# A selective-scan kernel whose `w` products move to 64-row bands, two states per pass and interleaved by column

## The chip, the cores and the metric

The kernel runs as one program on one core of one Trainium2 chip. The metric is device time in microseconds (us), the median of several runs; less is better. TensorE, VectorE, ScalarE, GpSimd and the DMA engines work side by side and meet at semaphores.

## What is computed

A pre-norm block in two stages, all in fp32, on x of shape (2, 2048, 256): first a selective scan, then a routed mixture of eight experts.

```
x = x + scan_layer(layernorm(x))
x = x + experts(layernorm(x))          # argmax of 8 logits picks one expert per token

scan_layer: dt = softplus(...); A = -exp(log_A)              # D = 256 channels, N = 16 states
  h[t] = exp(dt*A) * h[t-1] + (exp(dt*A) - 1)/A * x[t] * B[t,n]
  y[t] = sum over n of h[t] * C[t,n]; return y + D_skip * x
```

The kernel rewrites the recurrence. With v[t] = x[t]·B[t,n] and w[t] = v[t] − v[t−1], it runs h' = (h' + w)·a, a = exp(dt·A), so that VectorE's scan instruction has two operands: `w`, and `a`. The `w` of a state n is a product on TensorE of x (tokens by channels) with a banded matrix that has B[t,n] on its diagonal and −B[t,n] one column to its right.

## The kernel before

**Chunks, items, pairs.** Tokens are worked in eight chunks q of 512 (TC), each in four blocks of 128 tokens (TI). Channels are two halves h of 128. An item is one state n of one half h, all 512 tokens: 32 items per chunk (ITEMS), 256 in all, numbered g. Before, item g of a chunk has n = g // 2 and h = g % 2, so a pair (`m`) is one state in both halves.

**The stations of an item.** GpSimd builds the band of a state (`make_band`, L555: 128 x 516, that is four blocks of 129 columns), which both halves share. TensorE makes `w` (`make_w`, L921): four products, one per block of tokens, each with a full 128-row weight load of x and 129 columns of band streamed past it, into one PSUM bank of 512 columns. The 129th column spills into the next block and accumulates there. Each fp32 product stands in the trace as two weight loads and two matmuls, so an item has eight. There are NW = 4 such banks, item g uses bank g % 4. ScalarE makes `a` (`exp_a`, L741). VectorE scans (`scan`, L1110). Then h is multiplied by C/A: for most items on GpSimd (`make_hc`, L574), for which the scan writes to SBUF and ScalarE has scaled a copy of C (`copy_C`, L730); for the items of the states in VECTOR_N on VectorE (L1130), for which the scan works in place in PSUM. TensorE turns the result and adds it into YY (`add_y`, L939), four transpositions per item.

**What sets the order.** Every engine has its own program, written out by hand. TensorE's `emit(q)` goes over n = 0..15. In step n it makes `w` of items 2m+4 and 2m+5 and adds y of items 2m−4 and 2m−3, where m = 16q + n. `w` of item g waits until item g−4 has left its bank: the scan of g−4 where GpSimd multiplies, VectorE's product where VectorE does. For n < 2 and for the states on VectorE the two `add_y` stand ahead of the two `make_w`, otherwise behind. One small job per step (`fill`, a "hop": the layer norms' transpositions, projections, skip terms, routing) stands between. The hop tables give the skip terms u01 and u23 to steps 13 and 14 (L874) and the route to step 11.

**What VectorE does between scans.** `between(j, gap)` places its other work behind scan j of a chunk: `finish_rows` of the chunk before (L1168, two instructions behind each of scans 4 and 5; it waits until all y of that chunk are added), `ln2_stats` (behind 6 and 7), `dt_add` (L1137, behind 20 and 27), and `u_times_x` (L1158, two instructions behind each of scans 28 and 30; they wait for hop u01 and hop u23). In the last chunk u01 and u23 are hops 3 and 4 and are read behind scans 9 and 11. Hop u01 itself waits for `dt_add` behind scan 27, whose bank it takes.

**The rest.** After the eight chunks the expert stage runs 39 tiles of 128 tokens (hidden layer L1008, output L1024); the change does not touch it. Before the first chunk TensorE runs 80 small bf16 products (L964) and 24 products of 64 rows and 129 columns, by turns in the upper and the lower half of the array and in two banks (L967).

## Time and profile before

| | us |
|---|---|
| median of 3 runs | 805.61 (805.4 to 806.9) |
| the profiled execution | 804.56, its span 802.8 |
| first chunk starts on ScalarE (L690) | 25.2 |
| hidden layer of the experts starts (L1008) | 479.2 |
| TensorE busy, VectorE busy, GpSimd busy, ScalarE busy | 749.1, 546.2, 533.0, 461.3 |

A row of a timeline gives start, duration, engine, source line, operation and the tiles written and read; rows in a run are merged with a count. TensorE has two lines: PE for the matmuls, PEld for the weight loads that run under them. A matmul's shown duration contains its way through the array, so that its rate is read from start to start. A window row gives the busy time of each engine in a stretch and the clock that TensorE was granted in it, 1.00 being 2.4 GHz and 0.50 being 1.2 GHz.

### The profile page before, as it was taken

How to read it: one execution, taken by the hardware profiler on the slowest of the kernel's cores; microseconds unless marked ns; L12 is line 12 of the kernel's file. 1: busy time of each engine (PE TensorE's matmuls, PEld its weight loads, DVE VectorE, ACT ScalarE, POOL GpSimd, SP SyncE). 2: the span in 40 equal slices, each digit the busy share in tenths (PEclk: the TensorE clock that was granted, in tenths of full speed). 3: DMA queues.
4: the chain of work that ended last, by engine and by line, in shares of the span. 5: the costliest groups of instructions: out<-in, count | busy, mean ns of one | idle time of the engine just before them, and what ended most of it. 6: DMA issues, size and time to landing. Idle time of an engine off the chain costs nothing. (4 is left out here: it accounts for less than half of the span.)

```text
span 802.8 us, 17303 instructions
## 1 busy us (share of the span) xinstructions
PE 749.1 (93%) x5642; PEld 695.0 (87%) x5643; DVE 546.2 (68%) x914; ACT 461.3 (57%) x941; POOL 533.0 (66%) x654
## 2 busy tenths in 40 slices
PE   7899999999999997998998975969999999999993
PEld 5799999999899897898897975959999999999992
DVE  6889998989989989989789963353333334333430
ACT  3777898887888876876866753422332233223330
POOL 2799999989989986999898863552333343334420
PEclk9799999999999999998999987989999999999997
DMA  8666643233323331642844448341111111111000
GB/s 290 198 220 233 259 135 105 94 132 106 124 76 106 134 106 54 122 112 60 124 90 54 165 137 283 34 54 40 50 46 53 39 44 49 43 55 53 23 9 0
DMA packets 44375, 82.49 MB, mean 103 GB/s; under 512 B 6280, under 2 KB 14733, under 8 KB 44304
## 3 DMA queue, kind: packets, MB, share of 16 engines
q1 hardware_dynamic: 38288, 68.98, 29.2%
q0 software_dynamic: 6016, 12.61, 6.4%
q8 instruction: 38, 0.62, 0.3%
q14 instruction: 33, 0.27, 0.1%
HBM read 70.41 MB, written 13.91 MB: 105 GB/s over the span
## 5 line engine op out<-in xcount | busy, mean ns | idle before, releaser
L574 POOL TENSOR_TENSOR w_sb<-w_sb,Csb 128x512 f32<-128x512 f32 x182 | 231.7, 1275 | 41.2 <-DVE w_sb L1110 28.5
L921 PE MATMUL WW<-b_sb,xin 128*128 128x129 f32 (+1 forms) x1536 | 206.3, 284 | 8.3 <-DVE w_sb L1130 5.8
L921 PEld LDWEIGHTS WW<-b_sb,xin 128*128 128x128 f32 x1536 | 190.2, 197 | 24.0 <-issue 13.8
L812 ACT ACTIVATE dt<-WW,b1c 128x128 f32<-128x128 f32 x312 | 89.1, 369 | 191.8 <-PE WW L1008 191.8
L1110 DVE TENSOR_TENSOR_SCAN w_sb<-WW,hlast,w_sb 128x512 f32<-128x512 f32 x138 | 173.3, 1271 | 17.6 <-PE WW L921 17.2
L741 ACT ACTIVATE w_sb<-dt,negA 128x512 f32<-128x512 f32 x256 | 170.9, 710 | 18.7 <-DVE w_sb L1110 15.0
L1024 PE MATMUL misc<-w_sb,dt 128*128 x624 | 146.8, 390 | 9.1 <-issue 9.1
L634 POOL DMA_INDIRECT y_out<-CbX,ocol x39 | 46.8, 1201 | 150.5 <-DVE CbX L1418 149.9
L1024 PEld LDWEIGHTS misc<-w_sb,dt 128*128 128x128 f32 x624 | 119.5, 197 | 25.9 <-issue 10.1
L939 PE MATMUL YY<-sm,w_sb 128*128 128x128 f32 x1024 | 129.3, 276 | 0.1
L1008 PE MATMUL WW<-z,xin 128*128 128x128 f32 x624 | 120.7, 275 | 0.0
L939 PEld LDWEIGHTS YY<-sm,w_sb 128*128 128x128 f32 x1024 | 117.3, 144 | 0.3 <-POOL w_sb L574 0.3
L555 POOL TENSOR_TENSOR b_sb<-sm,brow 128x516 f32<-128x516 f32 x96 | 101.1, 1054 | 0.3
L730 ACT ACTIVATE Csb<-w_sb,invA 128x512 f32<-128x512 f32 x126 | 85.9, 713 | 26.4 <-POOL w_sb L574 26.2
L1415 DVE TENSOR_TENSOR CbX<-misc,b_sb 128x256 f32<-128x256 f32 x39 | 16.6, 425 | 118.0 <-PE misc L1024 118.0
L1008 PEld LDWEIGHTS WW<-z,xin 128*128 128x128 f32 x624 | 96.1, 192 | 0.9
L921 PEld LDWEIGHTS WW<-band,xin 128*128 128x128 f32 x512 | 63.2, 195 | 19.4 <-issue 10.8
L921 PE MATMUL WW<-band,xin 128*128 128x129 f32 (+1 forms) x512 | 68.7, 282 | 11.5 <-DVE w_sb L1130 11.5
L1110 DVE TENSOR_TENSOR_SCAN WW<-WW,hlast,w_sb 128x512 f32<-128x512 f32 x54 | 66.3, 1269 | 4.4 <-ACT w_sb L741 3.4
L1008 PE MATMUL WW<-z,xnT 128*128 128x128 f32 x320 | 62.0, 276 | 0.0
L1008 PE MATMUL WW<-z,Csb 128*128 128x128 f32 x304 | 58.8, 275 | 0.0
L1110 DVE TENSOR_TENSOR_SCAN w_sb<-WW,w_sb 128x512 f32<-128x512 f32 x44 | 52.9, 1212 | 5.6 <-PE WW L921 5.5
(214 smaller groups left out, 880.0 us busy)
## 6 DMA issues: line engine op xcount, KB each, us to landing
w_sb<-c_rows SPq DMA_DIRECT2D x86, 256.0 KB, 3.7
CbX<-c_rows SPq DMA_DIRECT2D x42, 256.0 KB, 3.5
w_sb<-w_in SPq DMA_DIRECT2D x20, 512.0 KB, 5.7
token_rows<-row SPq DMA_DIRECT2D x8, 1024.0 KB, 5.0
w_sb<-w_in SPq DMA_DIRECT2D x24, 256.0 KB, 6.6
xin<-x_in SPq DMA_DIRECT2D x8, 512.0 KB, 4.1
...
```

The lines of the kernel that those rows point to most:

```text
L555: eng.tensor_tensor(bands[m % NR], col("band").unsqueeze(1).to_broadcast([P, TI, BAND]), brow[q % B][:, :, N + n:N + n + 1].to_broadcast([ ...
L574: eng.tensor_tensor(hc[g % NHC], hb_of(g), Csb[i % NCS][:, :], ALU.mult).then_inc(s_hcp, 1)
L634: eng.indirect_dma_start(out=outrows, out_offset=bass.IndirectOffsetOnAxis(ap=ocol[u][:, :], axis=0), in_=yo[u], in_offset=None, bounds_ch ...
L730: eng.activation(Csb[i % NCS][:, :], Cb[m % NB], ACT.Copy, scale=invA[:, h * N + n:h * N + n + 1])\
L741: eng.activation(A[g % NA], dts[q % B][:, h * TC:(h + 1) * TC], ACT.Exp, scale=negA[:, h * N + n:h * N + n + 1]).then_inc(s_a, 1)
L812: g = eng.activation(hT[u % 2][:, j * P:(j + 1) * P], hps[u % 2][:, j * P:(j + 1) * P], ACT.Gelu, bias=b1c[u][:, j:j + 1])
L921: mm = eng.matmul(bank_of_w[:, i * P:i * P + width], x_rows[:, i, h * P:(h + 1) * P], bands[m % NR][:, i, 0:width], start=(i == 0), stop=( ...
L939: mm = eng.matmul(YY[:, at:at + P], hc[g % NHC][:, i * P:(i + 1) * P], ident, is_transpose=True, start=(j == 0 and i % 2 == 0), stop=(j == ...
L1008: mm = eng.matmul(hps[u % 2][:, j * P:(j + 1) * P], w1c[u % 2][h][:, j * P:(j + 1) * P], xT[u % 2][:, h * P:(h + 1) * P], start=(h == 0), ...
L1024: mm = eng.matmul(yps[u % 2][:, 0:D], hT[u % 2][:, j * P:(j + 1) * P], w2_sb[:, bass.ds(e * KH * D + j * D, D)], start=(j == 0), stop=(j = ...
L1110: eng.tensor_tensor_scan(hb_of(g) if pooled(g) else bank[g % NW], bank[g % NW], A[g % NA], hlast[(q - 1) % 2][:, h * N + n:h * N + n + 1] ...
L1415: eng.tensor_tensor(yo[u], yps[u % 2][:, 0:D], b2_sb[:, bass.ds(e * D, D)], ALU.add)\
```

## The change

Items are renumbered (`place`): a unit is now two neighbouring states n, n+1 of one half h, four items being (n, h0), (n+1, h0), (n, h1), (n+1, h1). A band is cut into blocks of 64 tokens and holds both states column by column: per 128 tokens 65 x 2 = 130 columns, so that one band of 128 x 520 serves four items. `w` of a unit lies interleaved in two PSUM banks (two units at a time, 1024 columns each), and the scan and VectorE's product read and write it at every second column. `make_w(m, part)` makes a unit in two parts. Part 0 has products of rows 0 to 63 into the first bank and of rows 64 to 127 into the second, by turns, and at its end one product of 2 columns for the spill across the bank's edge; part 1 has the halves the other way round, behind a wait for part 0. One `add_y` stands between the parts and one behind, the hop comes last, and all steps have this one order. On VectorE both products of a unit stand behind its second scan. VectorE's share goes from 37 pairs to 27 units; GpSimd's rises from 182 to 202 items.

```
-VECTOR_N = [(1, 3, 5, 8, 11, 13)] + [(1, 5, 8, 11)] * 4 + [(1, 3, 5, 8, 11)] * 2 + [(1, 4, 7, 10, 13)]
+VECTOR_UNITS = [(1, 6, 9, 12)] + [(1, 6, 11)] * 6 + [(1, 4, 7, 10, 13)]
-BAND = P + 1
-NR, NA, NH, NHC, NCS, NW, NB = 4, 4, 8, 8, 3, 4, 6
+HALF = P // 2
+BAND = 2 * (HALF + 1)
+NR, NA, NH, NHC, NCS, NW, NB = 3, 4, 8, 8, 3, 4, 6
...
+def place(g):
+    q, j = divmod(g, ITEMS)
+    return q, j // 4 * 2 + j % 2, j // 2 % 2
...
+        def unit(m):
+            return WW[:, m % 2 * 1024:(m % 2 + 1) * 1024]
+
+        def w_of(g):
+            return unit(g // 2).rearrange("p (t s) -> p s t", s=2)[:, g % 2, :]
...
-                eng.tensor_tensor(bands[m % NR], col("band").unsqueeze(1).to_broadcast([P, TI, BAND]),
-                                  brow[q % B][:, :, N + n:N + n + 1].to_broadcast([P, TI, BAND]), ALU.mult)\
-                   .then_inc(s_R, 1)
+                eng.tensor_tensor(bands[pair % NR].rearrange("p i (t s) -> p i t s", s=2),
+                                  col("band").unsqueeze(1).unsqueeze(3).to_broadcast([P, TI, HALF + 1, 2]),
+                                  brow[q % B][:, :, N + 2 * p:N + 2 * p + 2].unsqueeze(2)
+                                  .to_broadcast([P, TI, HALF + 1, 2]), ALU.mult).then_inc(s_R, 1)
...
+            def make_w(m, part):
...
+                pair, h = divmod(m, 2)
+                x_rows, band, to = xin[m // N % B], bands[pair % NR], unit(m)
+
+                def product(r, k, at=0, width=BAND, start=False):
+                    rows = slice(HALF * r, HALF * r + HALF)
+                    a = 2 * (P * k + HALF * r) + at
+                    return eng.matmul(to[:, a:a + width], x_rows[rows, k, h * P:(h + 1) * P],
+                                      band[rows, k, at:at + width], start=start, stop=not start, skip_group_check=True)
+
+                if part == 0:
+                    if h == 0:
+                        eng.wait_ge(s_R, pair + 1)
+                    if m >= 2:
+                        if pooled(2 * m - 4):
+                            eng.wait_ge(s_h, 2 * m - 2)
+                        else:
+                            eng.wait_ge(s_hc, vector_before(2 * m - 2))
+                    product(0, 0, start=True)
+                    product(1, 2, start=True)
+                    product(0, 1)
+                    product(1, 3, width=2 * HALF)
+                    product(1, 1, at=2 * HALF, width=2).then_inc(s_wf, 1)
+                else:
+                    eng.wait_ge(s_wf, m + 1)
+                    product(0, 2)
+                    product(1, 0)
+                    product(0, 3)
+                    product(1, 1, width=2 * HALF).then_inc(s_wv, 2)
...
-                    if n < 2 or n in VECTOR_N[q]:
...
+                    make_w(m + 2, 0)
+                    add_y(KD * m - 4)
+                    make_w(m + 2, 1)
+                    add_y(KD * m - 3)
+                    if n in at:
+                        fill(*at[n])
...
-                    if g % KD and not pooled(g) and KEPT[g // KD]:
-                        keep_h(g)
-                    if g and not pooled(g - 1):
+                    if g % KD and not pooled(g):
                         make_hc(g - 1)
+                        if KEPT[g // KD]:
+                            keep_h(g)
+                        make_hc(g)
```

How instructions stand on the engines, at three places. First TensorE in chunk 3, step 13, where hop u01 (two products of 17 rows, `misc<-sm,z`) stands; `h_ready` counts scans, `hC_ready` VectorE's products, `hC_ready_gpsimd` GpSimd's. Before:

```order
L921 MATMUL WW<-band,xin 128x129 [waits h_ready,band_ready]
L921 MATMUL WW<-band,xin 128x129 x2
L921 MATMUL WW<-band,xin 128x128
L874 MATMUL misc<-sm,z 128x256 [waits shared_bank_read_by_scalar,dt_ready]
L874 MATMUL misc<-sm,z 128x256
L921 MATMUL WW<-band,xin 128x129 [waits h_ready]
L921 MATMUL WW<-band,xin 128x129 x2
L921 MATMUL WW<-band,xin 128x128
```

and the same step after the change:

```order
L936 MATMUL WW<-b_sb,xin 128x130 [waits h_ready]
L936 MATMUL WW<-b_sb,xin 128x130 x2
L936 MATMUL WW<-b_sb,xin 128x128
L936 MATMUL WW<-b_sb,xin 128x2
L972 MATMUL YY<-sm,w_sb 128x128 [waits hC_ready]
L972 MATMUL YY<-sm,w_sb 128x128 x3
L936 MATMUL WW<-b_sb,xin 128x130 [waits w_of_first_halves]
L936 MATMUL WW<-b_sb,xin 128x130 x2
L936 MATMUL WW<-b_sb,xin 128x128
L972 MATMUL YY<-sm,w_sb 128x128 [waits hC_ready]
L972 MATMUL YY<-sm,w_sb 128x128 x3
L892 MATMUL misc<-sm,z 128x256 [waits shared_bank_read_by_scalar,dt_ready]
```

The hop stood behind one item's four products, which wait for scan 26; it now stands behind a whole unit and two `add_y`, and the first of these products waits for scan 27. On VectorE the reader of the hop (`tail<-misc`) stands where it stood, one scan behind `dt_add`; the rows of the changed kernel in chunk 1, where L1135 is the scan:

```order
L1135 SCALAR_TENSOR_TENSOR w_sb<-WW,hlast,w_sb 128x512 [waits hC_ready_gpsimd,a_ready,w_ready]
L1161 SCALAR_TENSOR_TENSOR dt<-misc,mag 128x512 [waits softplus_log]
L1135 SCALAR_TENSOR_TENSOR w_sb<-WW,hlast,w_sb 128x512 [waits h_last_kept,hC_ready_gpsimd,a_ready,w_ready]
L1182 SCALAR_TENSOR_TENSOR tail<-misc,vns,xin 128x256 [waits rstd_ahead,z_ready,shared_bank_filled]
L1182 SCALAR_TENSOR_TENSOR tail<-misc,vns,xin 128x256
L1135 SCALAR_TENSOR_TENSOR w_sb<-WW,hlast,w_sb 128x512 [waits hC_ready_gpsimd,a_ready,w_ready]
```

Here nothing moved. Last, TensorE in step 1 of chunk 4, where the last two y of chunk 3 are added. Before, the two `add_y` stand ahead, then a small hop, then `w`:

```order
L939 MATMUL YY<-sm,w_sb 128x128 [waits hC_ready_gpsimd]
L939 MATMUL YY<-sm,w_sb 128x128 x3
L869 MATMUL misc<-sm,cbrow 17x128 [waits cb_rows_ready,shared_bank_read_by_scalar]
L869 MATMUL misc<-sm,cbrow 17x128 x3
L921 MATMUL WW<-band,xin 128x129 [waits hC_ready,band_ready]
```

and after:

```order
L936 MATMUL WW<-b_sb,xin 128x130 [waits hC_ready]
L936 MATMUL WW<-b_sb,xin 128x130 x2
L936 MATMUL WW<-b_sb,xin 128x128
L936 MATMUL WW<-b_sb,xin 128x2
L972 MATMUL YY<-sm,w_sb 128x128 [waits hC_ready_gpsimd]
L972 MATMUL YY<-sm,w_sb 128x128 x3
L936 MATMUL WW<-b_sb,xin 128x130 [waits w_of_first_halves]
L936 MATMUL WW<-b_sb,xin 128x130 x2
L936 MATMUL WW<-b_sb,xin 128x128
L972 MATMUL YY<-sm,w_sb 128x128 [waits hC_ready_gpsimd]
L972 MATMUL YY<-sm,w_sb 128x128 x3
```

The last y of a chunk, for which `finish_rows` waits, now stands behind both parts of a `w` that itself waits for VectorE's products of unit 1.

## Rows read from the trace of the kernel before

**Rows 1.** The page's first part: busy us, share of the span, instructions.
```profile
PE 749.1 (93%) x5642; PEld 695.0 (87%) x5643; DVE 546.2 (68%) x914; ACT 461.3 (57%) x941; POOL 533.0 (66%) x654
```
**Rows 2.** Windows, one per chunk: us, busy us per engine (instructions), PE clock, DMA.
```profile
25.20:80.50 55.30, 51.38 (x390) 47.40 (x391) 49.38 (x58) 43.03 (x73) 51.51 (x68) 0.94 0.66 222
80.50:134.90 54.40, 54.22 (x446) 50.43 (x446) 50.54 (x66) 46.19 (x80) 50.17 (x59) 1.00 0.47 167
...
243.50:297.30 53.80, 53.75 (x445) 50.21 (x444) 49.34 (x71) 46.06 (x79) 48.69 (x58) 1.00 0.33 106
297.30:359.70 62.40, 58.17 (x463) 54.12 (x464) 57.06 (x80) 45.87 (x79) 52.70 (x61) 0.97 0.45 105
359.70:419.00 59.30, 55.66 (x429) 51.63 (x427) 51.97 (x77) 45.12 (x78) 55.48 (x64) 0.94 0.52 92
419.00:479.00 60.00, 52.49 (x412) 49.09 (x413) 53.59 (x78) 38.57 (x62) 49.02 (x52) 0.95 0.43 110
```
**Rows 3.** Groups by line of the whole span: count, busy us, mean ns, idle before.
```profile
L574 POOL TENSOR_TENSOR w_sb<-w_sb,Csb 128x512 f32<-128x512 f32 x182 | 231.7, 1275 | 41.2 <-DVE w_sb L1110 28.5 <-ACT Csb L730 11.7 <-PE misc L874 0.7
L1110 DVE TENSOR_TENSOR_SCAN w_sb<-WW,hlast,w_sb 128x512 f32<-128x512 f32 x138 | 173.3, 1271 | 17.6 <-PE WW L921 17.2
...
L555 POOL TENSOR_TENSOR b_sb<-sm,brow 128x516 f32<-128x516 f32 x96 | 101.1, 1054 | 0.3
```
**Rows 4.** Timeline of weight loads in chunk 3, 225 to 243 us: start, us, operation.
```profile
229.65 3.65 PEld L921 LDWEIGHTS WW<-b_sb,xin 128*128 128x128 f32 x32
233.23 0.91 PEld L939 LDWEIGHTS YY<-sm,w_sb 128*128 128x128 f32 x8
234.10 0.97 PEld L921 LDWEIGHTS WW<-band,xin 128*128 128x128 f32 x8
```
**Rows 5.** Timelines at the 64-row warm-up products, 7 to 10.5 us, and behind them.
```profile
7.62 2.95 PE L967 MATMUL WW<-tail 64*128 64x129 f32 x48
...
10.18 0.39 PE L967 MATMUL WW<-tail 64*128 64x129 f32 x4
...
10.50 0.14 PEld L845 LDWEIGHTS misc<-sm,xin 128*128 128x128 f32 x1
```
**Rows 6.** Timelines into and out of one skip-term hop, 184.7 to 186 us.
```profile
184.72 0.27 PE L921 MATMUL WW<-b_sb,xin 128*128 128x128 f32 x1
184.92 0.18 PEld L874 LDWEIGHTS misc<-sm,z 17*128 17x128 f32 x1
...
185.67 0.37 PE L874 MATMUL misc<-sm,z 17*128 17x256 f32 x1
185.98 0.19 PEld L921 LDWEIGHTS WW<-b_sb,xin 128*128 128x128 f32 x1 [0.33 <-issue]
```
**Rows 7.** Timeline of VectorE, 176 to 200 us: start, us, operation, count [idle before].
```profile
179.61 0.67 DVE L1137 SCALAR_TENSOR_TENSOR dt<-misc,mag 128x512 f32<-128x512 f32 x1
...
182.18 0.88 DVE L1158 SCALAR_TENSOR_TENSOR tail<-misc,vns,xin 128x256 f32<-128x256 f32 x2 [0.71 <-PE misc L874]
182.97 2.45 DVE L1110 TENSOR_TENSOR_SCAN w_sb<-WW,hlast,w_sb 128x512 f32<-128x512 f32 x2
...
192.77 0.72 DVE L1130 SCALAR_TENSOR_TENSOR w_sb<-WW,invA,w_sb 128x512 f32<-128x512 f32 x1
...
195.25 0.86 DVE L1168 SCALAR_TENSOR_TENSOR row<-YY,mvx,tail 128x256 f32<-128x256 f32 x2
...
199.18 0.72 DVE L1064 BATCH_NORM_STATS2 st<-row 128x6 f32<-128x256 f32 x2
```
**Rows 8.** Windows of 4 us in chunk 0: us, busy us per engine, PE clock, DMA.
```profile
28.00:32.00 4.00, 1.67 (x16) 1.38 (x15) 3.96 (x5) 1.76 (x4) 3.92 (x8) 1.00 0.62 197
32.00:36.00 4.00, 3.49 (x19) 3.26 (x18) 3.12 (x4) 4.00 (x8) 3.06 (x3) 0.54 0.37 88
```
**Rows 9.** Timeline at 477 us: two bf16 products of 96 columns, the second written strided.
```profile
477.23 0.29 PE L893 MATMUL misc<-onehot,tri_bf 128*128 128x96 bf16 x1
...
477.32 0.36 PE L894 MATMUL misc<-onehot,ones_bf 128*128 128x96 bf16 x1
```

130 lines of the change are left out of this document (51 added, 79 removed).

## The prediction

> **What bounds the kernel now.** First the page's busy line [rows 1]: TensorE is busy 93% of the span, VectorE 68%, but that is a mean over two stages. The change lies in the scan stage, 25 to 479 us, so I read the windows by chunk [rows 2]. In chunks 1 to 4 TensorE is busy all but 0.2 us of 54.4 us or less and VectorE 49 to 51: there TensorE is the bound. In chunks 5, 6 and 7 all of TensorE, VectorE and GpSimd are at 80 to 94% of their 59 to 62 us and wait for each other, and the clock is granted at 0.94 to 0.97. Then the pace of TensorE: an instruction of `w` comes every 3.58/32 = 0.112 us, one of y every 0.87/8 = 0.109 us [rows 4]. A unit of two items is 16 of the one and 8 of the other: 1.79 + 0.87 = 2.66 us, 42.6 us per chunk; the other 11.8 us of 54.4 are hops.
>
> **The concurrency is real.** The 24 warm-up products of 64 rows, by turns in the two halves and two banks, are the new `w` in small. Their 48 instructions take 2.88 us to the next kind's first load [rows 5]; without the way in and out (below) that is 0.055 us each, half of 0.112. So a part of four products costs 8 x 0.055 + 0.06 for the last to end = 0.50 us, two parts 1.00 instead of 1.79.
>
> **What the parts pay for it.** Each part is entered from and left to full-height work. The trace shows such borders. Into a hop of 17 rows: the last full matmul starts at 184.72, ends its columns 0.11 later (the step of [rows 4]), the next load starts only at 184.92 instead of under it, and takes another 0.11 until columns flow at 185.03: 0.20 lost. Out of it: 256 columns, twice as many, end at 185.67 + 0.21, load at 185.98, columns at 186.09: 0.20 [rows 6]. Out of the 64-row products into transpositions: the last matmul starts at 10.18 + 0.39 − 0.27 = 10.30, its columns end 0.11 later, the load comes at 10.50 and is 0.05 shorter: 0.15 [rows 5]. Every unit has four such borders: 2 x 0.20 + 2 x 0.15 = 0.70 us. The Trainium skill has this as a rule ("TensorEngine Tiling (Array Packing)", Key Properties: changing the tiling mode drains TensorE) without a price; the same page promises up to twice the speed for 64 rows, and by that alone a unit would lose 0.8 us.
>
> The product of 2 columns: its two instructions lie between 0.02 us (nothing but columns) and 0.22 us (two ordinary ones, 0.112 each). Its first load runs under the matmul ahead and its second doesn't, so I take 0.13.
>
> Sum for a unit on TensorE: 1.00 + 0.70 + 0.13 + 0.87 = 2.70 us against 2.66. The halving is eaten by the borders. Three hops per chunk are short-row work that now begins or ends at a 64-row part and saves a border each, 0.5 us. TensorE per chunk: 16 x 2.70 + 11.8 − 0.5 = 54.5 us, as before.
>
> **GpSimd.** 64 bands fewer at 1.054 = −67.5 us, 20 multiplications more at 1.275 = +25.5 us [rows 3]: 42 us less in the stage. The new band has 4 elements more but runs of two; no row shows that form. Between 1.05 us and the 1.28 us of a product with two full operands [rows 3]; I take 1.06. In either case GpSimd isn't the bound in chunks 1 to 4, and the gain counts in 5 to 7 only. ScalarE gets 20 copies of 0.71, 1.8 us per chunk, on 46 of 54 [rows 2]: hidden.
>
> **VectorE.** 20 products less; a scan steps on by 1.22 us, a product by 0.65, a skip-term pair takes 0.79, a `finish_rows` pair 0.78, statistics 0.65, `dt_add` 0.58 [rows 7] (shown times less the 0.07 to 0.09 by which neighbours overlap). About 1.3 us per chunk less. Scans and products now read every second column of PSUM. No row shows VectorE doing so. A scan takes 1.27 us for 512 columns, where the product, which reads the same bank, takes 0.72 [rows 3, 7]; a scan doesn't read PSUM as fast as it can be read, so I take no change; the bound on the other side is under the rivals.
>
> **The looser grip.** Before, `w` of an item waits for the item four back; from `w` ready to the next use of its bank TensorE has three items' work, about 5 us, and VectorE needs 1.2 of it. Now a unit waits for the unit two back, both scans done. From TensorE's start of a unit to `w` ready is about 2.3 us (part 0 0.6, border and y 0.6, border and part 1 0.7, the array 0.2, semaphores and first load 0.2), then VectorE takes 2.4; the bank is wanted again after 2 x 2.70 plus hops. That leaves 0.7 us where no hop stands. Any VectorE work above it stops TensorE. Three places per chunk do:
>
> 1. Start of a chunk. Unit 1 is VectorE's own and takes 2.4 + 1.3 + 0.1: 0.3 us of stop. Then the last y of the chunk before comes 2.9 us after unit 1 is done (all of step 1); VectorE has done scan 4 after 1.2 and waits 1.7 for it in `finish_rows`. Unit 2 is thus done at 2.9 + 0.8 + 1.2 = 4.9 us; TensorE was free at 2.7 + 0.4 for its hop: 1.8 idle. Unit 3 takes 0.8 + 1.2 + 0.65 + 1.2 = 3.85 against TensorE's 2.70: 1.15 idle; unit 4 another 0.2. Together 3.5 us.
> 2. Hop u01. It comes 2.7 + 1.05 + 0.15 = 3.9 us after scan 27. VectorE is there after `dt_add` and scan 28, 1.8 us, and waits 2.1 or more (0.71 before [rows 7]). TensorE has nothing else to do until scan 29: 0.8 + 1.2 + 0.05 = 2.05 idle.
> 3. Hop u23 and scan 31, the same: 2.05.
>
> That is 7.6 us per ordinary chunk, less the 0.2 that TensorE idles now. What hides none of it: after each of these points TensorE's next instruction in order is the `w` that waits.
>
> **Sum**, against the profiled execution's 804.6 us. Chunks 1 to 4: 4 x (7.4 + 0.1) = +30. Chunk 5: 54.5 + 7.5, and 2.2 more because token placing falls on unit 1, gives 64.2 against 62.4: +1.8. Chunk 6: 62 against 59.3: +2.6. Chunk 0 has no `finish_rows` and no route, but u01 and u23 (+4.1), less about 1.6 of waits for VectorE's own products, which are two states fewer: +2.5. Chunk 7 has its skip terms early, where no stop follows, pays the start (3.5) and gains from a lighter GpSimd: −1. The expert stage is unchanged. 804.6 + 36 = 840.5; the median stood 1 us above the profiled execution, so 840 to 841. **Forecast 840 us, slower by 4%.**
>
> **Rivals.**
> (a) Borders cost nothing here, because neighbouring loads slip under. A unit is 2.0 us, TensorE 43 us per chunk, and VectorE bounds: its 48 busy, 1.3 + 2.0 us of waits for the hops, 1 for `finish_rows`, some 2.5 behind long hops, 55 us. Chunks 1 to 4 stay within +1, chunks 5, 6 and 7 fall to about 58, 56 and 55, chunk 0 by 2: 805.6 − 10 = 796. Against it: two kinds of border in the rows show 0.15 to 0.20. This is the case on the faster side; it decides from a border below about 0.08 us. Chance 0.20.
> (b) Borders of half that: 2.35 per unit, chunks near 57 to 58: 805 to 822. 0.12, nearly all of it slower.
> (c) The forecast, 822 to 850: 0.48.
> (d) The new idle stretches let the clock fall. In chunk 0 TensorE was busy 1.67 of 4 us and the next 4 us ran at 0.54 of full speed, near 1.2 GHz [rows 8]. The stops at u01 and u23 leave it busy some 60% over 8 us, which is better than that. If it falls once in each chunk, 2 to 3 us each: 860. 0.12.
> (e) Strided PSUM reads slow the scan. The nearest row is TensorE's second bf16 product, 0.36 us for 96 columns written at a stride against 0.29 [rows 9], 0.7 ns per column. On 512 columns 0.37 us per scan, 12 us of VectorE per chunk, half of it beside TensorE: 885. The Trainium skill ("Advanced Engine Details and Errata", PSUM Cachelines) says that access to PSUM that isn't contiguous slows matmuls down much; of VectorE it says nothing. 0.06.
> (f) The halves don't overlap in the real `w` (same operands, real data): 16 x 0.112 + 0.70 + 0.13 + 0.87 = 3.5 us per unit, 13 us more per chunk than in (c): 940. 0.02.
>
> Faster by over 0.2%: (a) and a little of (b), 0.22; within 0.2%, about what a measurement can tell from no change, 0.04; slower 0.74. The range from 796 to 862 takes in (a) to (d) but for their ends.
>
> **What the changed profile would show.** Loads of the 64-row parts 0.055 apart, and a gap of 0.2 us at each change to and from y; if there is none, (a). A unit's 2.7 us from start to start in the middle of a chunk. VectorE waiting for TensorE 2 to 3 us ahead of each skip-term pair and 1.7 us ahead of `finish_rows` (by L1182 and L1192); if these are under 1 us, points 1 to 3 are wrong. Scans still 1.27 us, bands near 1.06. TensorE's clock at 1.00 in the middle of chunks. The stage's end near 515 us instead of 479, and the expert stage as long as before. The forecast is wrong above all if TensorE runs ahead at these places in a way that I missed, or if the two-column product costs more.

## The result: 13% slower, three times the loss that was forecast

The changed kernel takes 916.91 us (median of four runs, 904.6 to 925.7) against 805.51 for the kernel before. The times of the runs below are medians too, while the ratios leave out the slower executions of a kernel as a rule: the ratio here is 1.1285 (95% interval 1.1182 to 1.1387), by medians it is 1.138. The forecast was 840 with a range up to 862, so the sign was right and the size was not. The profiled execution is the fastest of the four, 904.62 us. In the four the time rises as the mean granted clock falls (0.877, 0.863, 0.856, 0.850), the first hint that the clock has a share in the loss.

The page's first part, to be read beside [rows 1]:

```profile
PE 791.9 (88%) x5898; PEld 667.1 (74%) x5899; DVE 535.2 (59%) x885; ACT 471.5 (52%) x961; POOL 495.2 (55%) x619
```

The windows, one per chunk and one for the expert stage, as in [rows 2] (us; busy us and instructions of TensorE, its loads, VectorE, ScalarE, GpSimd; clock; DMA):

```profile
25.70:94.80 69.10, 59.50 (x438) 46.31 (x438) 48.10 (x53) 45.81 (x77) 51.86 (x69) 0.75 0.60 201
94.80:162.20 67.40, 57.83 (x478) 45.37 (x478) 49.17 (x62) 47.15 (x81) 44.54 (x53) 0.89 0.35 119
162.20:230.70 68.50, 59.16 (x478) 46.57 (x478) 50.02 (x63) 47.17 (x81) 45.57 (x54) 0.87 0.26 86
230.70:301.30 70.60, 61.26 (x478) 48.31 (x478) 49.16 (x59) 47.19 (x82) 41.62 (x39) 0.84 0.25 83
301.30:373.00 71.70, 63.21 (x478) 49.76 (x478) 49.90 (x70) 47.05 (x81) 44.59 (x53) 0.81 0.26 82
373.00:446.00 73.00, 61.20 (x480) 48.11 (x480) 51.64 (x70) 47.28 (x81) 51.00 (x59) 0.83 0.31 81
446.00:514.40 68.40, 58.76 (x478) 46.38 (x478) 52.58 (x78) 47.45 (x82) 53.28 (x62) 0.87 0.35 79
514.40:578.00 63.60, 55.68 (x424) 45.43 (x424) 48.48 (x67) 37.13 (x61) 35.27 (x38) 0.80 0.36 111
578.00:902.80 324.80, 294.17 (x1990) 274.37 (x1990) 118.69 (x291) 96.16 (x322) 120.82 (x169) 0.96 0.21 55
```

The expert stage is as long as before (324.8 against 802.8 − 479.2 = 323.6). Nearly all of the loss lies in the chunks: 67 to 72 us in chunks 1 to 4 where before they took 54, and the clock is granted at 0.81 to 0.89 where it was 1.00 [rows 2]. No other engine is the bound: none is busy for more than 53.3 us of any chunk.

The groups that answer to [rows 3]. GpSimd's product and VectorE's scan are what they were, the new band takes 1.065 us against 1.054:

```profile
L593 POOL TENSOR_TENSOR w_sb<-w_sb,Csb 128x512 f32<-128x512 f32 x202 | 255.4, 1272 | 169.0 <-DVE w_sb L1135 111.6 <-ACT Csb L749 24.9 <-PE YY L972 13.3
L1135 DVE TENSOR_TENSOR_SCAN w_sb<-WW,hlast,w_sb 128x512 f32<-128x512 f32 x152 | 188.9, 1269 | 29.8 <-issue 28.6 <-PE WW L936 0.5
L574 POOL TENSOR_TENSOR b_sb<-sm,brow 128x520 f32<-128x520 f32 x64 | 68.1, 1065 | 0.4
```

The weight loads of one unit at 2.4 GHz, chunk 2 (start, us): part 0, y, part 1, y, and the next hop, to be read beside [rows 4]:

```profile
203.28 0.75 PEld L936 LDWEIGHTS WW<-b_sb,xin 64*128 64x128 f32 x10 [1.06 <-DVE w_sb L1154]
204.04 0.42 PEld L972 LDWEIGHTS YY<-sm,w_sb 128*128 128x128 f32 x4
204.63 0.53 PEld L936 LDWEIGHTS WW<-b_sb,xin 64*128 64x128 f32 x8 [0.17 <-issue]
205.27 0.42 PEld L972 LDWEIGHTS YY<-sm,w_sb 128*128 128x128 f32 x4
205.66 1.87 PEld L903 LDWEIGHTS misc<-sm,xnrT 128*128 128x128 f32 x16
```

2.38 us from the first load to the hop, and 0.17 to 0.2 more where a half follows instead: 2.6 us, where 2.70 was forecast. The halves do run side by side.

The waits of VectorE in the scan stage, 26 to 578 us (total, times, longest), by the line that waited:

```profile
DVE tail L1182 <- PE misc L892: 53.3, 15, 5.8
...
DVE row L1192 <- PE YY L972: 18.7, 7, 4.4
```

And the end of chunk 2, TensorE and VectorE; then the clock in windows of 4 us over the same stretch:

```profile
214.27 1.13 PE L892 MATMUL misc<-sm,z 17*128 17x256 f32 x4
215.43 0.88 DVE L1182 SCALAR_TENSOR_TENSOR tail<-misc,vns,xin 128x256 f32<-128x256 f32 x2 [3.96 <-PE misc L892]
...
217.64 0.83 PE L936 MATMUL WW<-b_sb,xin 64*128 64x130 f32 x10 [2.25 <-DVE w_sb L1135]
...
223.19 0.88 DVE L1182 SCALAR_TENSOR_TENSOR tail<-misc,vns,xin 128x256 f32<-128x256 f32 x2 [4.51 <-PE misc L892]
...
225.31 1.45 PE L936 MATMUL WW<-b_sb,xin 64*128 64x130 f32 x10 [2.16 <-DVE w_sb L1135]
```

```profile
214.00:218.00 4.00, 1.75 (x14) 1.15 (x13) 2.57 (x4) 0.86 (x2) 0.42 (x1) 1.00 0.20 64
218.00:222.00 4.00, 4.00 (x27) 3.17 (x25) 0.67 (x1) 2.31 (x4) 3.24 (x4) 0.65 0.00 0
222.00:226.00 4.00, 1.84 (x9) 1.03 (x9) 2.81 (x4) 0.00 (x0) 0.67 (x1) 0.50 0.10 26
226.00:230.00 4.00, 4.00 (x26) 3.43 (x24) 2.58 (x3) 0.00 (x0) 4.00 (x5) 0.50 0.48 175
230.00:234.00 4.00, 4.00 (x27) 3.58 (x25) 2.69 (x4) 3.29 (x7) 0.21 (x1) 0.50 0.00 0
```

The stops stand where the prediction put them: VectorE waits for u01, then TensorE stands 2.25 us; the same at u23. But behind the first one the clock goes to 1.2 GHz, and it stays there for 16 us. At that clock a unit takes 4.6 us (255.03 to 259.67 in the trace of e3, below), and VectorE waits longer for the next hop: in chunks 0 to 5 it waits 3.9 to 5.8 us for u23. For u01, ahead of the fall, it waits 2.5 to 2.7 us, as forecast; only in chunk 2, the one shown, is it 3.96, and there a first short stretch at 1.2 GHz (208 to 212 us) lies ahead of it, right behind the route hop (205.8 to 207.5).

To compare kernels I counted the windows of 2 us with a clock under 0.75 in the scan stage: how many stretches of them, how long together, and the longest. The kernel before has 4 stretches, 26 us in all, the longest 8. The changed kernel has 16, 186 us in all, the longest 26.

### The profile page after: what moved, and what is told of

It is laid out like the page before. It is cut to its first block and busy times, and to the rows that moved or that the text cites. A ratio compares the mean times of both kernels' runs of the same rounds, so it can differ in the third digit from the quotient of the medians.

```text
span 902.8 us, 17676 instructions
## 1 busy us (share of the span) xinstructions
PE 791.9 (88%) x5898; PEld 667.1 (74%) x5899; DVE 535.2 (59%) x885; ACT 471.5 (52%) x961; POOL 495.2 (55%) x619
## 5 line engine op out<-in xcount | busy, mean ns | idle before, releaser
L593 POOL TENSOR_TENSOR w_sb<-w_sb,Csb 128x512 f32<-128x512 f32 x202 | 255.4, 1272 | 169.0 <-DVE w_sb L1135 111.6
L936 PEld LDWEIGHTS WW<-b_sb,xin 64*128 64x128 f32 x2304 | 196.6, 221 | 143.8 <-issue 91.4
L936 PE MATMUL WW<-b_sb,xin 64*128 64x130 f32 (+2 forms) x2304 | 234.6, 326 | 74.3 <-DVE w_sb L1135 63.6
L1135 DVE TENSOR_TENSOR_SCAN w_sb<-WW,hlast,w_sb 128x512 f32<-128x512 f32 x152 | 188.9, 1269 | 29.8 <-issue 28.6
L972 PE MATMUL YY<-sm,w_sb 128*128 128x128 f32 x1024 | 193.6, 320 | 0.0
L972 PEld LDWEIGHTS YY<-sm,w_sb 128*128 128x128 f32 x1024 | 124.6, 157 | 20.4 <-issue 6.5
L1050 PEld LDWEIGHTS misc<-w_sb,dt 128*128 128x128 f32 x624 | 119.3, 196 | 26.1 <-issue 10.5
L574 POOL TENSOR_TENSOR b_sb<-sm,brow 128x520 f32<-128x520 f32 x64 | 68.1, 1065 | 0.4
L1135 DVE TENSOR_TENSOR_SCAN w_sb<-WW,w_sb 128x512 f32<-128x512 f32 x50 | 59.0, 1208 | 12.1 <-issue 7.5
L1135 DVE TENSOR_TENSOR_SCAN WW<-WW,hlast,w_sb 128x512 f32<-128x512 f32 x40 | 50.1, 1281 | 17.8 <-ACT w_sb L759 9.1
L749 ACT ACTIVATE Csb<-CbX,invA 128x512 f32<-128x512 f32 x66 | 44.9, 711 | 15.3 <-POOL w_sb L593 15.1
L1034 PEld LDWEIGHTS WW<-z,xnT 128*128 128x128 f32 x320 | 49.8, 192 | 1.6 <-issue 0.8
```

The costliest lines, as they stand in the source:

```text
L574: eng.tensor_tensor(bands[pair % NR].rearrange("p i (t s) -> p i t s", s=2), col("band").unsqueeze(1).unsqueeze(3).to_broadcast([P, TI, HA ...
L593: eng.tensor_tensor(hc[g % NHC], hb_of(g), Csb[i % NCS][:, :], ALU.mult).then_inc(s_hcp, 1)
L749: eng.activation(Csb[i % NCS][:, :], Cb[m % NB], ACT.Copy, scale=invA[:, h * N + n:h * N + n + 1])\
L936: return eng.matmul(to[:, a:a + width], x_rows[rows, k, h * P:(h + 1) * P], band[rows, k, at:at + width], start=start, stop=not start, ski ...
L972: mm = eng.matmul(YY[:, at:at + P], hc[g % NHC][:, i * P:(i + 1) * P], ident, is_transpose=True, start=(j == 0 and i % 2 == 0), stop=(j == ...
L1034: mm = eng.matmul(hps[u % 2][:, j * P:(j + 1) * P], w1c[u % 2][h][:, j * P:(j + 1) * P], xT[u % 2][:, h * P:(h + 1) * P], start=(h == 0), ...
```

## The experiments

**Theory at the start:** the stops named in the prediction, made dearer by the clock that falls behind them. **Rivals:** the borders of the half-array work or the two-column product cost more than taken; VectorE's waits hide something that is late anyway. Ratios are to the kernel before on the same chip, since its own time there was between 804 and 814 us. The last three columns are of the one execution that was traced.

| kernel | ratio (95%) | by medians | traced, us | shortest of chunks 1 to 4, its clock | at 1.2 GHz: stretches, us, longest |
|---|---|---|---|---|---|
| before | 1 | 1 | 804.6 | 53.8, 1.00 | 4, 26, 8 |
| changed | 1.128 (1.118 to 1.139) | 1.138 | 904.6 | 67.4, 0.89 | 16, 186, 26 |
| e1 hops first | 1.080 (1.069 to 1.090) | 1.078 | 864.0 | 58.3, 0.97 | 13, 152, 44 |
| e2 y first | 1.093 (1.083 to 1.103) | 1.103 | 912.4 | 67.2, 0.86 | 13, 222, 30 |
| e3 both | 1.018 (1.012 to 1.024) | 1.027 | 845.6 | 58.3, 0.94 | 9, 116, 42 |
| e4 filler | 1.117 (1.109 to 1.124) | 1.111 | 888.8 | 62.8, 1.00 | 10, 118, 26 |
| e5 full height | 1.118 (1.114 to 1.122) | 1.119 | 903.4 | 65.8, 1.00 | 16, 66, 8 |
| e7 before, new order | 1.058 (1.054 to 1.062) | 1.060 | 854.9 | 61.5, 1.00 | 2, 16, 8 |
| e8 parts together | 1.030 (1.026 to 1.033) | 1.031 | 833.0 | 56.3, 1.00 | 8, 78, 18 |
| e10 lighter VectorE | 1.032 (1.024 to 1.040) | 1.031 | 826.8 | 55.6, 1.00 | 7, 86, 22 |
| e11 full height, both | 1.033 (1.028 to 1.038) | 1.032 | 831.7 | 58.9, 1.00 | 2, 8, 6 |
| e12 route later | 1.052 (1.048 to 1.057) | 1.053 | 853.4 | 61.2, 0.94 | 11, 110, 16 |

### e1 to e3: take the stops away

e1 puts hops u01 and u23 ahead of the step's first part:

```
+                    first = q + 1 < NQ and n in (13, 14)
+                    if first:
+                        fill(*at[n])
                     make_w(m + 2, 0)
...
-                    if n in at:
+                    if n in at and not first:
                         fill(*at[n])
```

> The changed kernel, but hops u01 and u23 stand ahead of the first part of w in steps 13 and 14 instead of behind the whole step; nothing else. Changed kernel: 917 us (905 to 926 in its runs). Theory T (stops of TensorE, with the clock falling to 1.2 GHz behind them): the waits of VectorE ahead of the skip terms (L1182, 53 us in all) fall under 15 us, the half-clock stretch at the end of each chunk shrinks, and the time falls by more than the 2 x 2.05 x 7 = 29 us of the stops themselves: to 850 to 880. Rival 1 (the borders of the array mode or the two-column product cost the excess, not the stops): 885 to 890 at best, since only the stops go. Rival 2 (VectorE's waits there are filled by work that is late anyway): no change, above 905.

Measured: 877.3 us (864.0 to 885.6), inside theory T's 850 to 880. VectorE's wait ahead of the skip terms falls from 53.3 to 10.9 us, and the shortest chunk takes 58.3 us with the clock at 0.97. Time at 1.2 GHz falls less, from 186 to 152 us, so these two stops aren't all that brings the clock down.

e2 puts both `add_y` ahead in steps 0 and 1:

```
+                    if n < 2:
+                        add_y(KD * m - 4)
+                        add_y(KD * m - 3)
                     make_w(m + 2, 0)
-                    add_y(KD * m - 4)
+                    if n >= 2:
+                        add_y(KD * m - 4)
```

> The changed kernel, but in steps 0 and 1 of a chunk both add_y stand ahead of the two parts of w; nothing else. Theory T: the wait ahead of finish_rows (18.7 us in all) falls under 5 us, TensorE's stops at units 2 to 4 shrink from 3.5 to about 1.5 us per chunk, and the time falls by 7 x 2 to 7 x 5 us, to 880 to 900, the more since the clock comes back earlier. Rival 1 (border costs): 903 or more. Rival 2: y ahead now holds w back (it waits for GpSimd's products) and the stop only moves: 910 to 925.

Measured: 897.5 us (882.7 to 912.4), inside theory T's 880 to 900 by its median. The wait ahead of `finish_rows` falls from 18.7 to 2.2 us; that ahead of the skip terms rises to 66.4.

e3 is both.

> Both of the two edits above. Theory T: the three stops of a chunk that the prediction named are gone or small, the clock stays near 2.4 GHz through chunks 1 to 4, chunks fall from 67 to 73 us to about 56 to 58: 805 to 835 in all. Rival 1 (the excess lies in the borders and in w itself): chunks stay above 62 us, 870 or more. The edits together should give more than the sum of the two alone if the clock needs both stops gone.

Measured: 836.1 us (825.7 to 845.6), VectorE's wait ahead of the skip terms down from 53.3 to 10.7 us and ahead of `finish_rows` from 18.7 to 1.3. Theory T had 805 to 835, rival 1 870 or more. Against the changed kernel e1 takes 0.049 off the ratio, e2 0.036, together 0.085; both edits in one kernel take 0.111 (by medians 0.060, 0.036 and 0.111). So each of the two orders holds part of the loss; that they make each other dearer is likely by the ratios and not clear by the medians. The rival by which the excess lies in borders and in `w` itself falls: e3 has all of these, and of the loss of 12.8% there are 1.8% left (2.7% by medians, of 13.8%). Two windows of e3's traced execution, 845.6 us and so above its median, show what is left. Chunk 2 takes 58.25 us at a clock of 0.94, chunk 3 takes 71.5; this is chunk 3 cut in two:

```profile
206.80:243.00 36.20, 31.78 (x300) 24.90 (x299) 30.49 (x38) 31.67 (x56) 26.55 (x26) 1.00 0.33 104
243.00:278.30 35.30, 35.30 (x181) 27.88 (x180) 19.28 (x23) 15.63 (x26) 16.69 (x16) 0.52 0.19 60
```

300 instructions of TensorE in the first 36 us, 181 in the next 35. In the second piece TensorE is busy without a gap, and the clock stays at 1.2 GHz from 244 us to the chunk's end.

### e4: keep the order, hold the clock up

Small bf16 products into a free bank, where TensorE stands still, in chunks 0 to 4. No other instruction's wait changes; those of steps 14 and 15 wait themselves until VectorE has read the bank.

```
+            def busy(b, q, n):
...
+                for i in range(24 if n > 3 else 16):
+                    eng.matmul(misc[b][:, 0:P], ones_bf[:, :], ones_bf[:, :], start=True, stop=True)
...
+                    if q < 4 and n in (14, 15):
+                        busy(0 if n == 14 else 1, q, n)
+                    if 0 < q < 5 and n in (2, 3):
+                        busy(1, q, n)
```

> The changed kernel in its own order, with small bf16 products (24 or 16 of 128 columns, into a free bank) put where TensorE stands still: ahead of steps 14 and 15 in chunks 0 to 3 and of steps 2 and 3 in chunks 1 to 4. They change no wait and no result. 24 of them take 1.3 us at 2.4 GHz and 2.6 at 1.2. If the clock is the missing term (T): it stays higher in chunks 1 to 4, and these fall from 67 to 73 us towards 62 to 64: 885 to 900 in all. If the clock is no cause, or idle time of 2 us doesn't lower it: the same or up to 10 us slower than the changed kernel, 915 to 930.

Measured: 904.6 us (888.8 to 912.9), between the two expectations, 885 to 900 and 915 to 930; the ratio is 1.117 against 1.128, by medians 1.111 against 1.138, and the traced execution takes 888.8 us where that of the changed kernel took 904.6. In all that is little, since chunk 4 has few fillers, chunks 5 to 7 none and the expert stage none, but the chunks with them separate the two parts of the loss. Chunks 1 to 3, then chunk 5, which has none:

```profile
90.35:155.37 65.02, 59.84 (x558) 47.64 (x559) 49.34 (x63) 47.26 (x82) 44.51 (x54) 0.95 0.43 138
155.37:218.15 62.78, 56.79 (x558) 45.69 (x559) 49.44 (x63) 47.28 (x82) 44.52 (x54) 1.00 0.30 94
218.15:282.13 63.98, 58.29 (x558) 46.66 (x558) 49.13 (x60) 47.23 (x81) 42.80 (x41) 0.97 0.26 92
...
349.73:423.87 74.14, 63.24 (x480) 49.94 (x480) 51.66 (x70) 47.36 (x82) 51.11 (x59) 0.80 0.30 79
```

With the clock at 1.00 the changed kernel's chunk takes 62.8 us. The prediction's sum for it was 61.9 (54.4 + 7.4 + 0.1). VectorE's waits with the clock held are those of the prediction too: 2.60 and 2.72 us ahead of that chunk's skip terms, 1.56 ahead of its `finish_rows`, which stands in the next chunk:

```profile
207.02 0.88 DVE L1194 SCALAR_TENSOR_TENSOR tail<-misc,vns,xin 128x256 f32<-128x256 f32 x2 [2.60 <-PE misc L892]
212.98 0.88 DVE L1194 SCALAR_TENSOR_TENSOR tail<-misc,vns,xin 128x256 f32<-128x256 f32 x2 [2.72 <-PE misc L892]
...
224.39 0.88 DVE L1204 SCALAR_TENSOR_TENSOR row<-YY,mvx,tail 128x256 f32<-128x256 f32 x2 [1.56 <-PE YY L972]
```

So of the changed kernel's 67.4, 68.5 and 70.6 us in chunks 1 to 3, some 62.8 is structure (order, units and borders at full clock) and 4.6 to 7.8 is the clock.

### e5: the same stops, full height

```
-                    rows = slice(HALF * r, HALF * r + HALF)
+                    rows = slice(0, P)
```

> The changed kernel, but every product of w takes all 128 rows instead of 64: the same number of products, columns, parts and waits, no change of the array's mode at the parts' edges, and no work side by side. The output is wrong (a block of w gets the sum over 128 tokens, not 64); only the time counts. By the rows of before a unit is 16 x 0.112 + 0.13 + 0.87 = 2.79 us on TensorE against 2.60 in the changed kernel's trace. In the runs so far the stretches at 1.2 GHz were 12 to 42 us long with the halves, though TensorE was busy in all of them, and 4 to 8 us in the kernel before. Theory C (work in halves, or its borders, keeps the clock down once it is down): the stops at the hops and at the chunk's start stay, but the clock returns within 4 to 8 us behind each, and the time is 860 to 890, below the changed kernel's 917 in spite of more work per unit. Theory S (the stops alone keep it down, whatever the work): the clock is as low as in the changed kernel, and 0.2 us more per unit give 930 to 950.

Measured: 902.6 us (899.4 to 903.9), neither theory's number. On the clock it sides with theory C: the stops are all there (1.81, 2.25 and 2.16 us in each of chunks 1 and 2), 16 times the clock falls, but no stretch is longer than 8 us and the clock is 0.93 to 1.00 in chunks 1 to 4. The same stops don't always bring it down: the chunk at 1.00 has all three. On the time theory C was 13 to 43 us too low; it had not counted that with the clock back the stops still cost what they cost. At the full clock the two can be compared: 65.8 us for a chunk here, 62.8 in e4. Halving is worth 3.0 us per chunk, 0.19 per unit, as long as the clock stays. The total says what it is worth with the clock: 1.118 at full height, 1.128 in halves, with intervals that overlap (by medians 1.119 and 1.138). It gives nothing, and costs 1 to 2% if the middles are right.

### e7: the old `w`, the new order

The kernel before, with `w`, y, `w`, y, hop in every step:

```
+                    make_w(KD * m + 4)
+                    add_y(KD * m - 4)
+                    make_w(KD * m + 5)
+                    add_y(KD * m - 3)
+                    if n in at:
+                        fill(*at[n])
```

> The kernel before with the step order of the changed one: w, y, w, y, hop, in every step. No halves, items and grip as before. Theory: w of an item waits there for one scan and not for two, with four items of reach, so the late hops and the late last y cost less: 1 to 3 us per chunk, 815 to 835 us with before at 806 to 814, and the clock comes back within 8 us of each stop. Rival: the order alone makes the change's loss: 870 or more. Second rival: no loss at all, then the stops need the unit of two states.

Measured: 854.4 us (851.7 to 854.9), more than the theory's 815 to 835 and less than the first rival's 870. Two of its chunks:

```profile
86.77:149.28 62.51, 56.23 (x445) 50.25 (x445) 51.12 (x66) 46.31 (x79) 49.93 (x59) 1.00 0.43 146
149.28:211.79 62.51, 56.23 (x445) 50.24 (x445) 51.12 (x66) 46.32 (x79) 49.97 (x59) 1.00 0.30 94
```

62.5 us at 1.00, where the kernel before takes 54.4 [rows 2] and the changed one with its clock held 62.8. The order by itself, without units, halves or the grip of two units, costs 8.1 us in chunks 1 and 2 and 7.3 and 7.7 in chunks 3 and 4. That is about as much as the changed kernel loses by structure, 8.4. And the clock stays at 1.00 in chunks 1 to 6, although TensorE is idle for 5.4 to 10.3 us of each. These aren't the stops of the changed kernel: behind u01 and u23 TensorE stands 0.63 us here, where it stood 2.25 and 2.16, and the longest stop of an ordinary chunk is 1.69. But chunk 5 has stops of 2.37, 1.46, 1.69 and 1.96 us within 14 us (they end at 340.0, 343.0, 347.6 and 351.6), and the clock holds there as well. So a stop of this length doesn't bring the clock down by itself.

### e8, e10, e12: can the halves be made to pay?

e8 is e3 with the two parts back to back and both `add_y` behind, so two borders per unit instead of four.

```
                     make_w(m + 2, 0)
-                    if n >= 2:
-                        add_y(KD * m - 4)
                     make_w(m + 2, 1)
                     if n >= 2:
+                        add_y(KD * m - 4)
                         add_y(KD * m - 3)
```

> The kernel with both edits (hops u01 and u23 first, y first in steps 0 and 1; 836 us), and in all steps the two parts of w back to back, then both add_y. Two borders per unit instead of four, 0.35 us less per unit by the prediction, but the wait for part 0 is then open: its last product's way through the array, about 0.2 us. If borders cost what the prediction took and hold the clock down: 815 to 832. If the wait costs as much as the borders: 832 to 842, no change. If y so late starves GpSimd's buffers: slower.

Measured: 831.4 us (828.7 to 833.0). That is where the two expectations meet (815 to 832, and 832 to 842 for no change). Against e3 it is no gain: 1.030 and 1.018 by the ratio, 1.031 and 1.027 by medians. The undisturbed chunks are shorter, 56.3 us at 1.00, and three of the eight at 64 us lose it again.

e10 gives unit 1 to GpSimd in chunks 1 to 6:

```
-VECTOR_UNITS = [(1, 6, 9, 12)] + [(1, 6, 11)] * 6 + [(1, 4, 7, 10, 13)]
+VECTOR_UNITS = [(1, 6, 9, 12)] + [(6, 11)] * 6 + [(1, 4, 7, 10, 13)]
```

> The kernel with parts together and both edits (831 us), and in chunks 1 to 6 only units 6 and 11 on VectorE, unit 1 on GpSimd too. VectorE's start of a chunk is 1.3 us shorter and TensorE's first unit waits for scans alone; GpSimd gets 2.55 us more on 45 of 56. If the grip of VectorE on TensorE at the chunk's start is what is left: 1 to 2 us per chunk and a better clock, 815 to 826. If GpSimd's buffers now hold VectorE back there: 831 or slower.

Measured: 829.0 us (823.2 to 834.2), above the 815 to 826 expected and by the ratio no better than e8. Chunks at full clock take 55.6 to 56.1 us, 0.7 less than in e8, and chunks 2, 5 and 6 fall to the low clock. Chunks 2 and 3:

```profile
137.32:200.56 63.24, 58.21 (x478) 47.12 (x477) 48.51 (x60) 48.07 (x83) 47.58 (x57) 0.87 0.30 93
200.56:256.17 55.61, 50.65 (x478) 41.23 (x477) 47.74 (x57) 47.82 (x83) 44.56 (x42) 1.00 0.31 105
```

The same work, 7.6 us apart by the clock. All three falls came within 4 us of the start of the route hop, whose sixteen instructions stream 8 columns each and which stands 6 us behind a stop of 1.6 us; in chunks 1, 3 and 4 the same stop and the same hop bring no fall. The first fall of e3 (128 us, its hop at 124.8) and three of e8 (the first at 184.9, its hop at 181.9) stand there too, while the kernel before runs this hop in chunks 1 to 4 without a fall. e12 moves it a step on:

```
-            at |= {8: ("xnr0", q - 1), 9: ("xnr1", q - 1), 11: ("route", q - 1)}
+            at |= {8: ("xnr0", q - 1), 9: ("xnr1", q - 1), 12: ("route", q - 1)}
```

> The kernel of e10 (parts together, both edits, lighter VectorE; 829 us), with the route hop (16 products of 8 columns, 1.85 us) in step 12 instead of step 11. In e10's trace the clock fell in chunks 2, 5 and 6 right behind this hop, which came 6 us after a stop of 1.6 us at dt_add; the chunks in which it didn't fall take 55.6 us, the others 63 to 67. If the stop and the short products together make it fall: it falls in fewer chunks, 805 to 822. If only the stop or only the hop does: no change, 825 to 835. Even at 2.4 GHz throughout it would not be under the kernel before, since 55.6 us is above its 54.4.

Measured: 853.2 us (850.4 to 864.7), slower than e10 and outside both expectations. VectorE reads the route behind scan 26 and now waits 2.67 us for it; hop u01, which waits for VectorE's `dt_add`, holds TensorE 2.5 us more; the clock falls in each of chunks 1 to 6, within 1 us of this new stop's end. The stop of 1.6 us is still there too, so this run doesn't tell what made the clock fall in e10. And even e10's best chunk, 55.6 us, is above the 54.4 of before: with these two-unit banks TensorE and VectorE, 50.7 and 47.7 us busy, still wait for each other. No version with halves beat the kernel before.

### e11: both edits, full height

> The kernel with both edits (hops first, y first; 836 us), but every product of w at full height, as in e5 (a wrong sum in w, the same counts and waits). A unit costs 0.2 us more at 2.4 GHz. Theory C (halves with their borders don't bring the clock back): the clock is 0.96 or more in chunks 1 to 4 and no stretch at 1.2 GHz is longer than 8 us; chunks 57 to 59 us, 825 to 840 in all, no slower than the halves in spite of more work. If halves cost no clock once the stops are gone: 6 x 16 x 0.2 = 20 us or more slower than e3, 855.

Measured: 830.4 us (829.9 to 831.7), as theory C expected. The edit is that of e5 on e3. Chunks 1 to 4 take 58.9 to 59.5 us, all at 1.00, and there are two low stretches of 8 us together in the whole stage, against 116 in the trace of e3. But the two kernels don't have the same stops: with its dearer units e11 has none above 0.68 us in chunks 1 to 4, while e3 still has stops of 1.04 to 1.64 us there, and in chunk 3 the clock falls behind the one of 1.57. So this pair doesn't tell whether the halves or the stops that they leave take the clock; only e5 against the changed kernel, with equal stops, speaks for the halves. By medians the halves (836.1 with before at 813.9, 1.027) and full height (830.4 with before at 804.3, 1.033) are about 0.5% apart, and by the ratios of the table 1.5%, at most 12 us; at a clock that held, 3.0 us per chunk would give 24. So half or more of what halving earns is lost again even with both orders mended.

### e6, e9, e13: the clock and the borders by themselves

Four, five and five tests on TensorE alone, each behind a stop. Their program is a list of calls; the halves and the full-height parts are those of the kernel:

```
+            stop(1)
+            for i in range(40):
+                halves_part(0)
+            stop(2)
+            for i in range(24):
+                halves_part(0)
+                turns()
...
```

> The changed kernel with four tests on TensorE put before the first chunk, each behind a stop of about 5 to 10 us: 40 parts in halves without anything between; 24 times a part in halves and four transpositions; 24 parts at full height, and right behind them, at whatever clock they leave, 24 times the mix of halves and transpositions; 20 times a part at full height and four transpositions. Theory C1 (halves alone keep the clock down): the first test stays at 1.2 GHz for over 10 us. Theory C2 (the borders do): the first test gets to 2.4 GHz as fast as the full-height one, the mix doesn't. Theory S: all four get to 2.4 GHz after the same few us. If a mix entered at 2.4 GHz stays there for 30 us, halves don't lower the clock, they only fail to bring it back. At 2.4 GHz the mix gives the price of a border: a part and four transpositions of 0.50 + 0.44 us without borders, 1.29 with the predicted 0.35. The time is not compared.

Measured: all four tests were back at 2.4 GHz 4.5 to 6.1 us after TensorE went to work again, and the mix that was entered at 2.4 GHz stayed there for its 30 us. In this run halves neither lower the clock nor keep it down, as theory S expected and against C1 and C2; but each test was run once. The price of a border comes from the loads of the mix at 2.4 GHz, a part in halves and four transpositions by turns:

```profile
62.36 0.52 PEld L1004 LDWEIGHTS WW<-sm 64*128 64x128 f32 x8 [0.19 <-issue]
63.00 0.42 PEld L1016 LDWEIGHTS YY<-sm 128*128 128x128 f32 x4
63.59 0.52 PEld L1004 LDWEIGHTS WW<-sm 64*128 64x128 f32 x8 [0.17 <-issue]
64.24 0.42 PEld L1016 LDWEIGHTS YY<-sm 128*128 128x128 f32 x4
```

and from the window of pure halves, 184 instructions in 10 us, 0.054 each:

```profile
30.00:40.00 10.00, 10.00 (x184) 10.00 (x182) 0.00 (x0) 0.00 (x0) 0.00 (x0) 1.00 0.01 3
```

8 × 0.054 + 0.44 for four transpositions (their step beside full-height parts in the last test) is 0.87; a turn takes 1.23. Two borders are 0.36 us, where 0.35 was forecast.

e9 runs units, `units(count, full height, two-column product, wait between parts, hop)`, on the expert weights:

```
+            units(12, False, False, False)
...
+            units(16, False, True, False)
...
+            units(16, False, True, True)
...
+            units(16, False, True, True, True)
...
+            units(16, True, True, True)
```

> The changed kernel with five tests on TensorE put behind its last tile, each behind a stop of some us, on the expert weights as data: (1) 12 units of two parts in halves, each followed by four transpositions; (2) 16 units with the two-column product added; (3) the same, with the wait between the parts as in the kernel; (4) the same, with two 17-row products of 256 columns behind every second unit; (5) 16 units as in (3), but at full height. In the first bench all mixes came back to 2.4 GHz 6 us after TensorE went to work again, though the scan stage has stretches of 16 to 42 us at 1.2 GHz with TensorE always busy. If it is the real unit (its two-column product, its wait, or real data) that doesn't bring the clock back, one of tests 1 to 4 stays at 1.2 GHz for over 10 us and test 5 doesn't; the first of them that does names the cause. If all come back in 6 us, the cause is in the waits for other engines between units, or in the hops. The time is not compared.

Measured: tests 1, 2, 3 and 5 came back after 4.2 to 5.9 us of work, test 4, with the 17-row hop, after 17 us. That pointed to thin hops between halves, in one test of five. But the first hop of test 4 comes only 9.3 us after its start, and up to there it is the same as test 3, which was back after 5.9.

e13 has other hops in the same frame:

```
+            units(12, True, True, True, "rows17")
...
+            units(12, False, True, True, "rows17")
...
+            units(12, False, True, True, "short")
...
+            units(12, False, True, True, "turns")
...
+            units(12, True, True, True, "short")
```

> As e9, with five other tests behind the last tile, 12 units each, with a hop behind every second unit: (1) full height with two 17-row products of 256 columns, (2) halves with the same, (3) halves with 16 products of 8 columns, (4) halves with four full transpositions, (5) full height with 16 products of 8 columns. In e9 halves without hops were back at 2.4 GHz 5 to 6 us after work began, halves with the 17-row hop after 17. If it needs both, halves and thin hops: (1) and (4) come back in about 6 us, (2) again takes over 10, (3) too. If thin hops alone do it: (1) and (5) take over 10 too. If the 17 us in e9 was chance: (2) comes back in 6. The time is not compared.

Measured: (1), (2) and (4) were back in 3.9 to 5.3 us, so that e9's 17 us with the 17-row hop was not repeated and is not explained by it. But with products of 8 columns, halves (3) stayed at 1.2 GHz for 37 us, and then went up and down; at full height (5) the clock was back in 3.9 us, and fell again 3 to 4 us after the start of each of its six hops, for 3 to 7 us each time (the last to the test's end). TensorE was busy throughout. (The hop here is 32 instructions of 8 columns, twice the kernel's route.) The low stretch of (3), then the rest of (3), and all of (5):

```profile
1041.00:1078.00 37.00, 36.89 (x198) 32.96 (x200) 0.06 (x1) 0.00 (x0) 0.00 (x0) 0.50 0.00 1
1078.00:1114.00 36.00, 36.00 (x305) 32.48 (x303) 0.00 (x0) 0.00 (x0) 0.00 (x0) 0.85 0.00 1
1178.00:1245.00 67.00, 67.00 (x493) 67.00 (x493) 0.00 (x0) 0.00 (x0) 0.00 (x0) 0.80 0.00 1
```

The hops don't explain the start of (3). Its first instruction, the last transpositions ahead of its first hop, and the hop:

```profile
1041.11 1.24 PE L1094 MATMUL WW<-w_sb 64*128 64x130 f32 x8 [13.04 <-DVE scr L1528]
...
1049.36 1.11 PE L1102 MATMUL YY<-sm,w_sb 128*128 128x128 f32 x4
1050.26 1.93 PE L1122 MATMUL YY<-w_sb 128*128 128x8 f32 x9
```

For 9 us there are halves and transpositions only, the same instructions as at the start of (2) and (4), and the clock doesn't come back. So one and the same start in units of halves was made five times, in e9 (3) and (4) and e13 (2), (3) and (4): three times the clock was back after 5.1 to 5.9 us, twice it was not back after 9. The starts at full height, five in all, took 3.9 to 5.9 us.

## Why the prediction was wrong in size

**The pace of TensorE** held: 2.6 us per unit for 2.70, borders 0.18 us each for 0.15 to 0.20, the two-column product near 0.12 for 0.13 (0.76 us for ten loads, 0.64 for eight). The Trainium skill ("TensorEngine Tiling (Array Packing)", Key Properties) says that changing the mode drains TensorE; this case's trace agrees, with a gap of 0.17 us at each such change, and the price is what the rows before had shown. Rivals (a), (b) and (f) were wrong.

**Scans and bands** held: 1.269 and 1.065 us. VectorE's scan is no slower for reading every second column of PSUM, 1.269 us against 1.271. What the Trainium skill ("Advanced Engine Details and Errata", PSUM Cachelines) says of matmuls doesn't carry over to it here; rival (e) was wrong.

**The stops** held in place and in size: 2.60, 2.72 and 1.56 us of waits with the clock at 1.00 (e4), and a chunk of 62.8 for 61.9. Their cause was told wrongly in one point. The prediction laid all of them on the looser grip, two units instead of four items. e7 has the old grip and loses 7.3 to 8.1 us per chunk by the order of the step alone, so the order is enough for a loss of this size. What the grip adds shows with the order mended: e11's chunks 1 to 4 take 59.2 us in the mean, all at 1.00, against 54.2, of which 16 × (2.79 − 2.66) = 2.1 is the dearer unit, and some 2.9 are left for the grip. That last figure is a difference of differences and no more than an estimate.

**The clock** is the step that failed. The sum had no term for it, and rival (d) gave it 2 to 3 us in each chunk and a chance of 0.12, on the argument that TensorE stays busy some 60% over 8 us. The trace shows TensorE busy 5.75 of 8 us at u01 (214 to 222 us), more than that 60%, and the clock at 1.2 GHz for 16 us all the same. Laid side by side with the forecast: chunk 0 took 69.1 for 57.8 (+11.3), chunks 1 to 4 278.2 for 247.6 (+30.6), chunk 5 73.0 for 64.2 (+8.8), chunk 6 68.4 for 62 (+6.4), chunk 7 63.6 for 59 (+4.6): 61.7 us, and 840.5 + 61.7 is 902.2 of the profiled 904.6. Of chunks 1 to 4 the clock is 4.6 to 8.9 us each, 27 us of the 30.6, if all four have the 62.8 us of e4's chunk at 1.00. For chunks 0, 5, 6 and 7 the split between clock and structure was not measured; their clocks of 0.75 to 0.87 and e7's 66.9 us for chunk 5 at a clock of 1.00, above the 64.2 that the prediction had, suggest that both take part.

Why one fall costs so much has three parts. At 1.2 GHz a unit takes 4.6 us for 2.6, and TensorE is the bound. The late hop comes later still (waits for u23 of 3.9 to 5.8 us instead of 2.7), so the next stop follows while the clock is still down. And with the same stops the stretches at 1.2 GHz are up to 26 us long with the halves and 8 at full height (e5).

**What stays open:** what brings the clock down, and why it comes back so late with halves. A stop of 2.2 us stands right ahead of a fall in each of chunks 0 to 6 of the changed kernel, but in e5 the same stops once brought none, in e7 four stops of 1.46 to 2.37 us in a row brought none, and in e13 the clock fell with TensorE busy. Units of halves came back in 5.1 to 5.9 us in three tests and in two were not back after 9 us, with no hop yet. Products of 8 columns brought a fall each time in e13, at full height too, and the kernel has half such a hop once per chunk; but some of the long stretches of the changed kernel, as that of 220 to 236 us, don't begin at it. The share of each hop was not settled, and two late returns in five are too few to say how often halves cause one.
